# Masked attention of sixteen small heads: the row of maxima leaves between the pairs' stacks, score places chosen by which comes free first, and the outputs of four heads transposed in halves of 64 rows

## The reference, cut to what matters

```python
# the first of eight layers; x is (1, 1024, 256), HEADS = 16, so a head has 16 columns
q = (x @ Wq).reshape(B, T, H, Dh)
k = (x @ Wk).reshape(B, T, H, Dh)
v = (x @ Wv).reshape(B, T, H, Dh)
scores = jnp.einsum('bthd,bshd->bhts', q, k)
mask = jnp.tril(jnp.ones((T, T), dtype=scores.dtype))
scores = scores * mask
attn = jax.nn.softmax(scores / T ** 0.5, axis=-1)
out = jnp.einsum('bhts,bshd->bthd', attn, v).reshape(B, T, H * Dh)
return out @ Wo
...
x = x + _L0_attn_a_ref(_layernorm(x, axis=-1), Wq, Wk, Wv, Wo)   # then seven more layers
```

## Time and profile before

| | us |
|---|---|
| median of 3 runs | 2227.73 (2225.84 to 2228.39) |
| the profiled execution | 2225.98 |
| its span, first to last instruction | 2224.2 |
| the attention layer's last instruction, within the span | about 248 |
| first query unit, first key unit on PE | 41.99, 97.22 |

### The profile page before, as it was taken

How to read it: one execution, slowest core, us unless ns; L and a number is a source line. 1 busy time by engine, 2 the same in 40 slices (tenths; PEclk the granted TensorE clock), 3 DMA queues, 4 the chain that set the end, 5 groups by cost and what they waited for, 6 DMA issues and landing times. The chain is left out here.

```text
span 2224.2 us, 33777 instructions
## 1 busy us (share of the span) xinstructions
PE 1929.2 (87%) x11770; PEld 1552.0 (70%) x11770; DVE 1345.6 (60%) x2478; ACT 936.7 (42%) x1655; POOL 703.4 (32%) x570
## 2 busy tenths in 40 slices
PE   6399799879964667996699999999999999998898
PEld 4144488758841225885588888888888888886687
DVE  4365444655458994346577776767676776674443
ACT  2165343324333323334355554545454554553332
POOL 3001133114348642333433333323233332230132
PEclk9699799889978887997699999999999999999799
DMA  3400013111300002321000000000000000000232
GB/s 80 73 2 2 29 45 108 38 29 53 108 6 0 1 0 85 106 76 52 8 6 11 7 7 10 10 10 10 10 10 10 7 10 10 7 6 15 83 111 78
DMA packets 44908, 73.87 MB, mean 33 GB/s; under 512 B 7360, under 2 KB 27456, under 8 KB 44800
## 3 DMA queue, kind: packets, MB, share of 16 engines
q1 hardware_dynamic: 44800, 72.56, 11.2%
HBM read 64.87 MB, written 1.25 MB: 30 GB/s over the span
## 5 line engine op out<-in xcount | busy, mean ns | idle before, releaser
L791 ACT ACTIVATE gqa_probs<-acc,gqa_bias,gqa_q_scale 128x128 f32<-128x128 f32 (+7 forms) x256 | 212.5, 830 | 274.3 <-DVE gqa_bias L882 274.0
L337 POOL TENSOR_TENSOR f_weighted<-f_hidden,f_comb_all 128x512 f32<-128x512 f32 x128 | 190.5, 1490 | 416.7 <-DVE f_hidden L400 345.1
L1050 PE MATMUL aux<-gqa_probsT,gqa_v 128*128 128x128 f32 x2304 | 306.8, 279 | 1.4 <-ACT gqa_oT L813 1.4
L878 DVE TENSOR_REDUCE gqa_neg_max<-acc 128x1 f32<-128x128 f32 (+7 forms) x256 | 193.7, 757 | 176.4 <-PE acc L1017 165.7
L1050 PEld LDWEIGHTS aux<-gqa_probsT,gqa_v 128*128 128x128 f32 x2304 | 283.7, 195 | 8.2 <-issue 5.1
L734 POOL TENSOR_TENSOR gqa_q_high<-gqa_straight,gqa_turned_q 128x512 fp32r<-128x512 f32 x64 | 81.6, 1275 | 514.7 <-DVE gqa_turned_q L839 514.7
L477 PE MATMUL aux<-xnT_high,f_w_high 128*128 128x512 f32 x512 | 213.8, 418 | 20.6 <-ACT f_silu_g L358 11.1
L400 DVE TENSOR_TENSOR f_hidden<-f_silu_g,aux 128x512 f32<-128x512 f32 x128 | 87.9, 687 | 230.2 <-ACT f_silu_g L358 124.7
L477 PE MATMUL aux<-xnT_low,f_w_high 128*128 128x512 f32 x512 | 210.8, 412 | 0.0
L477 PE MATMUL aux<-xnT_high,f_w_low 128*128 128x512 f32 x512 | 209.9, 410 | 0.0
L1034 PE MATMUL aux<-ident,gqa_probs 128*128 128x128 f32 x1152 | 179.9, 280 | 7.9 <-DVE gqa_probsT L910 4.6
(11 more groups left out here) (330 smaller groups left out, 4325.9 us busy)
## 6 DMA issues: line engine op xcount, KB each, us to landing
f_comb_all<-comb_by_expert SPq DMA_DIRECT2D x48, 512.0 KB, 4.0
f_w<-in_f_up SPq DMA_DIRECT2D x64, 256.0 KB, 3.6
f_w<-in_f_down SPq DMA_DIRECT2D x64, 128.0 KB, 3.8
mat_qk<-mat_high SPq DMA_DIRECT2D x64, 64.0 KB, 2.3
gqa_w_q<-in_g_wq SPq DMA_DIRECT2D x32, 128.0 KB, 2.1
gqa_wo<-in_g_wo SPq DMA_DIRECT2D x32, 128.0 KB, 2.1
mat_qk<-mat_low SPq DMA_DIRECT2D x32, 64.0 KB, 2.3
stream<-in_x SPq DMA_DIRECT2D x1, 1024.0 KB, 5.8
```

The costliest lines, as they stand in the source:

```text
L337: pool.tensor_tensor(weighted[:, j % SLOTS], hidden[:, j % SLOTS], comb_all[:, j // 2 % 2, j % 2 * HALF:(j % 2 + 1) * HALF], ALU.mult).the ...
L791: act.activation(probs[:, j % 4, 0:width(j)], scores(j), ACT.Exp, bias=bias[:, j % 16:j % 16 + 1], scale=q_scale[:, j // NT % 2, tile_of(j ...
L878: dve.tensor_reduce(neg_max[:, j % 16:j % 16 + 1], scores(j), AX, ALU.max, negate=True).then_inc(max_ready, 1)
L1050: last = pe.matmul(aux[:, 2 + t // 4, t % 4 * P:(t % 4 + 1) * P], v[:, g, s, :], probsT[:, j % 4, s * P:(s + 1) * P], start=(s == 0), stop ...
```

## The change

Three things are edited. First, SP issues the stacks of pairs 0 to 2, then waits for the row of pair 0, issues it, issues the stack of pair 3, waits for the row of pair 1, and so on. Second, the function `places()` gives each step the place which, by a small running model of PE, DVE and ACT times, comes free first, and `before` records which step had it. Third, the turning works on halves of 64 rows: 16 transposes of 64 x 128, each with 64 columns of the identity, so that one ACT copy per four heads suffices; the waits on `out_copied` are counted in ones for it.

```diff
     steps = order()
-    slotted = [x for x in steps if x[0] in ("query", "key", "row", "turn", "chunk", "project")]
+    def places():
+
+        place, before, had, left = {}, {}, [None] * 3, [0.0] * 3
+        pe = dve = act = 0.0
+        for kind, n in steps:
+            if kind in ("masked", "weigh"):
+                pe += 0.6
+            if kind == "save":
+                act += 0.6
+            if kind not in ("query", "key", "row", "turn", "chunk", "project"):
+                continue
+            i = left.index(min(left))
+            place[kind, n], before[kind, n], had[i] = i, had[i], (kind, n)
+            pe = max(pe, left[i])
+            if kind == "query":
+                t, c = q_units()[n % UNITS]
+                wide = min((t + 1) * P, (c + 1) * HALF) - c * HALF
+                pe += 0.2 + 0.0004 * wide
+                dve = left[i] = max(dve, pe) + 0.1 + 0.0021 * wide
+            elif kind == "key":
+                b, c = k_units()[n % UNITS]
+                wide = (c + 1) * HALF - max(b * P, c * HALF)
+                pe += 0.2 + 0.0004 * wide
+                act = left[i] = max(act, pe) + 0.2 + 0.0017 * wide
+            else:
+                pe += 0.2 if kind == "row" else 1.0
+                act = left[i] = max(act, pe) + (0.3 if kind == "row" else 1.0)
+        return place, before
...
-        place = {x: i for i, x in enumerate(slotted)}
+        place, before = places()
 
         def slot(kind, n):
-            return slots[place[kind, n] % 3]
+            return slots[place[kind, n]]
...
-            for p in range(PAIRS):
+            def stack(p):
                 sp.wait_ge(low_ready, 2 if p < PAIRS // 2 else 4)
...
+            for p in range(3):
+                stack(p)
             for p in range(PAIRS):
                 sp.wait_ge(row_ready, p + 1)
...
+                if p < PAIRS - 3:
+                    stack(p + 3)
...
-                    for h in range(4):
-                        act.activation(out[:, :, 4 * n + h, :].rearrange("p (c j) d -> p c j d", c=2),
-                                       slot("turn", n)[:, h // 2, :].rearrange("p (j c g d) -> p g c j d", j=4, c=2, g=2)[:, h % 2, :, :, 0:HD0 + 1],
-                                       ACT.Copy).then_inc(out_copied, 1)
+                    act.activation(out[:, :, heads(n), :],
+                                   flat(slot("turn", n)).rearrange("p (t h d) -> p t h d", t=NT, h=4)[:, :, :, 0:HD0 + 1],
+                                   ACT.Copy).then_inc(out_copied, 1)
...
             def free(kind, n):
 
-                i = place[kind, n]
-                if i < 3:
+                if before[kind, n] is None:
                     return
-                was, m = slotted[i - 3]
+                was, m = before[kind, n]
...
-                for t in range(NT):
-                    last = pe.transpose(flat(slot("turn", n))[:, t * P:(t + 1) * P], outT_head[:, t * P:(t + 1) * P], core.ident[:, :])
+                for a in range(2):
+                    for j in range(4):
+                        for c in range(2):
+                            rows = slice(64 * c, 64 * c + 64)
+                            last = pe.transpose(slot("turn", n)[:, c, j * P + 64 * a:j * P + 64 * a + 64],
+                                                outT_head[rows, a * HALF + j * P:a * HALF + (j + 1) * P], core.ident[rows, rows])
```

More of the change, by code:

```diff
@@ L1322, in _ @@
                     break
-                pool.wait_ge(out_copied, 4 * g + 4)
+                pool.wait_ge(out_copied, g + 1)
                 pool.wait_ge(masked_weighed, 2 * g + 2)
@@ L1426, in _ @@
             dve.wait_ge(masked_weighed, 8)
-            dve.wait_ge(out_copied, 16)
+            dve.wait_ge(out_copied, 4)
             dve.tensor_tensor(cut, cut, out[:, :, heads(3), HD0:HD0 + 1].rearrange("p t h a -> p t (h a)"), ALU.add).then_inc(denominator, 1)
@@ L1486, in free @@
                 elif was == "turn":
-                    pe.wait_ge(out_copied, 4 * m + 4)
+                    pe.wait_ge(out_copied, m + 1)
                 elif was == "chunk":
```

## The result

The median fell from 2227.67 (2225.84 to 2228.39, 4 runs) to 2189.12 us (2184.74 to 2190.95, 4 runs): ratio 0.9825 [0.9808, 0.9842]. Forecast were 2195.0 (2188 to 2203) and -32.7 us.

What follows compares the result with a forecast made beforehand. SP's queue was taken to bound the 33.7 us wait, PE the stretch from 106 to 235 us. Terms -32.4 + 0.8 - 0.3 + 0 - 0.6 - 0.2 = -32.7 us gave 2195.0 us, range 2188 to 2203.

Steps and rivals of the forecast that it cites:

- The wait and its cause: First key unit waits 33.7 us for pair 0's row, held in SP's queue; with the row earlier, it starts near 63.6.
- What is late next: After the first key unit, DVE backlog and pair 3's stack together cost 1.2 us; query 23 moves by -32.4 us.
- DVE backlog: Two DVE reductions from 63.44 to 65.25 us; query 20 starts no earlier than that.
- The clock: PE's full clock returns perhaps 4 us of work later, counted from the first key unit: +0.8 us.
- at most 0.36 us: Worth on PE of each microsecond at half the clock, from eight weigh instructions at 1.64 and 1.05 us.
- rival 4: The clock doesn't come back: PE stays at half from the first key units, +40 us, 2268 us; chance 3%.
- The places: Four key units gain 0.7 us each, six queries lose 0.41 us each: -0.3 us; bounds -4.4 and +2.5.
- The turning: Sixteen half transposes cost the same as eight whole ones in each of four turnings: 0, bounds -2.2 to +4.4 us.
- The lower bound, 0.55: Time per turning if two half transposes run side by side and the columns set the time: 0.55 us.
- The copies: One ACT copy of 0.63 us replaces four of 0.81 per turning: -0.6 us on PE's path, -0.2 at the end.
- The sum: All terms together, reaching the layer's end: -32.7 us, median 2195.0 us.
- Rival 3: The places do more: waits for maxima gone (-4.1) and transposes at 0.55 (-2.2), 2188.7 us; chance 9%.

Runs made afterwards that it cites:

- e1_queue: The kernel before with only the new order on SP (stacks of pairs 0 to 2, row 0, stack 3, ...): 2197.74 us, ratio 0.9859.
- e9_own_ring: The changed kernel with exponentials of key units 2 and 3 in memory that no stack is copied from: 2185.28 us, one run.
- e7_swap: The changed kernel with queries 35, 47, 59, 71, 83 and 95 given the place that comes free second: 2187.34 us, ratio 0.9826.
- e2_places: The kernel before with only the new places: 2227.86 us, ratio 0.9998.
- e12_again: The changed kernel once more, with no edit: 2189.05 us, ratio 0.9832.
- e5_act_row: The changed kernel with ACT issuing both row transfers behind its copy and SP issuing all stacks in one loop: 2194.77 us, ratio 0.9857.
- e10_two_first: The changed kernel with only the stacks of pairs 0 and 1 ahead of the row of pair 0: 2196.06 us, one run.
- e4_no_places: The changed kernel with its places going round in turn again: 2191.77 us, ratio 0.9833.
- e8_warm: e5_act_row with two matmuls of zeros on PE behind each of query units 8 to 17: 2195.13 us, ratio 0.9860.
- e11_swap_ring: The changed kernel with the edits of e7_swap and e9_own_ring together: 2186.64 us, ratio 0.9826.
- e3_turning: The kernel before with only the halves of 64 rows and the one copy per turning: 2222.51 us, ratio 0.9981.

## Why the prediction was right, and where a size was off

- **The wait and its cause.** As forecast: the row left at 59.94, the first key unit stood at 62.95 (63.6 forecast) without a wait. e1_queue shows that the order on SP does it alone.
- **What is late next.** Exponential 2 at 70.68 (70.9 forecast), waiting for a transfer; query 23 at 72.46 (72.8), so -32.73 where I had -32.4. The wait for the stack alone costs 1.24 us by e9_own_ring; forecast were 1.2 for it and the DVE backlog together, and the backlog cost nothing that the runs show.
- **The clock.** Forecast +0.8 us, because the small gaps would bring the clock back some 4 us later. In after it came back 7.3 us behind the first key unit where it was 7.1 before, so this cost some 0.1 us and the reason given did not show. But the term is real: in e7_swap the same code up to there got its clock back 13.0 us behind key 0 and paid 1.61 us by query 24. The size in any one execution is luck; the "at most 0.36 us" for each microsecond at half was too low: the runs give 0.45 where exponential 2 has no long wait. Full long before 80 us, and no swing until 200: rival 4 did not come. The section of the Trainium skill named in the prediction, page "TensorE: Matmul & The Clock Gate", has short idle gaps between groups of matmuls as what makes the clock swing. The fall at 56.6 us again follows such gaps (PE busy 1.92 of 3.00 us in 54 to 57), and it did not recur in 88 to 200 us, where PE is busy 107.14 of 112.00.
- **The places.** Forecast -0.3, measured -0.04 between query 24 and key 95 (e2_places): -0.65 and the losses stand at the units that the forecast named, and e7_swap confirms the +0.41. The forecast left out key 1, which now waits for the exponential of key 0; exponential 2 stands 4.20 instead of 3.78 us behind key 0 in e2_places, and this is the likely cause of the 0.2 us at query 24.
- **The turning: the term that was mis-sized.** I took 0, from "eight pairs at the price of eight single ones". The step on PE shrank from 1.02 to 0.53 us, three times in the middle, and at the last turning the copy comes 204.80 - 204.05 = 0.75 us behind the first transpose instead of 240.05 - 238.94 = 1.11: some -1.85 us in all. The lower bound, 0.55, was met, but not quite for its reason: the two halves of a pair do start side by side, half the columns take 0.58 of the time, and the next unit starts 0.17 us sooner behind them, which the sum did not have. The copies were right, 0.62 us instead of 0.81. The Trainium skill, page "TensorEngine Tiling (Array Packing)", section "Key Properties", has the parallel row tiles, and the trace agrees: the halves of a pair start within 0.01 us. By its section "Instruction Overhead" (some 60 cycles for each matmul) half the columns save less than half; the transposes' own steps agree, 0.063 against 0.109 us, and only with the sooner start of the next unit does the whole step come to 0.52 of 1.02.
- **The sum.** Up to layer 2 -36.08 us against the -32.7 forecast: of the 3.4 us between them 1.85 are the transposes, 0.4 the earlier first key unit (34.03 against 33.6), 0.45 the delays and the clock (1.55 against 1.2 + 0.8), 0.24 lie ahead of row 0 and some 0.6 at the layer's end, and the places take 0.3 back. The 0.6 can't be called a gain of the change: the same code took 13.77 us there in one execution and 15.37 in the other (e12_again), at another clock. A further -1.81 us lies in layers whose code did not change. Rival 3's 2188.7 is nearest to the 2189.12 measured, and that is half luck: its transposes came (-1.85 for its -2.2), its places (-4.1) did not, and what makes up for them lies mostly outside the sum.
- **Those layers.** Windows from about 1099 us behind the start of layer 2 to the start of the last layer, after:

```profile
1314.00:2012.32 698.32, 672.11 (x4511) 589.29 (x4511) 470.48 (x1090) 347.98 (x656) 196.76 (x151) 0.96 0.03 9
```

and the same stretch in e12_again, the same kernel:

```profile
1315.30:2008.26 692.96, 667.31 (x4511) 584.99 (x4510) 469.62 (x1088) 347.62 (x654) 195.37 (x149) 0.97 0.03 9
```

and in e2_places:

```profile
1351.00:2053.92 702.92, 679.15 (x4512) 594.01 (x4511) 472.52 (x1092) 349.62 (x656) 198.64 (x152) 0.95 0.03 8
```

The same instructions take 693 to 703 us at a granted clock of 0.97 to 0.95. The two executions of the changed kernel are 5.4 us apart (1797.15 and 1791.72, the second below the 1794 to 1802 that I had expected), so the -1.81 us is within what repeats of one kernel show. Open stays whether part of it is systematic: the three profiles with the old queue have 1798.96, 1801.62 and 1798.15 us from layer 2 to the last, the eleven with the row moved 1791.7 to 1800.9, with a mean some 3 us lower.

## What to carry to other kernels

A transfer whose data are made early can still leave late: compare the line of the trace that makes the data with the line that issues it on its queue, and count what stands between them. When it is moved ahead, what it is moved past becomes the next thing waited for, and its price is the time by which it lands behind its first use, minus what the engines have to do meanwhile. Moving the issue to a compute engine is no way out where that engine's next results are waited for: 2.04 us of issuing on ACT per pair came back as waits of PE. A rule that picks the place which comes free first gains where a unit waited and loses as much where it takes a place just before its reader is done; look at both kinds before expecting anything of it.

## What the runs showed of the hardware that I had not expected

- Half transposes, f32, in rows 0 to 63 and 64 to 127: the two halves start together, a pair takes 0.063 us against 0.109 for a whole one; sixteen halves with the step to the next unit 0.53 us, eight whole ones 1.02.
- The clock falls in some executions where it holds in others, in the same code: in 42 to 54 us the granted clock was 1.00 in before, after and four more executions, 0.86 in two (e5_act_row, e10_two_first) and 0.72 in six (e1_queue to e4_no_places, e8_warm, e11_swap_ring), with PE busy as long:

```profile
42.00:54.00 12.00, 10.75 (x76) 8.03 (x76) 7.10 (x8) 2.23 (x4) 7.15 (x14) 1.00 0.58 102
```

for after, and for e1_queue:

```profile
42.00:54.00 12.00, 10.75 (x57) 7.76 (x57) 6.41 (x7) 1.20 (x2) 7.19 (x15) 0.72 0.60 104
```

Row 0 stands at 58.6 to 59.5 us in the six with the full clock, at 60.4 and 60.9 in the two and at 61.9 to 64.3 in the six. With the new order on SP these three microseconds pass into the whole program; in e2_places and e3_turning, with the old order, they vanish in the wait for the row (key 0 at 97.91 and 97.13, 97.22 before). That is why the pieces of the layer were compared and not the medians.
- When the clock comes back after such a fall differs too, and here it could be priced: some 0.45 us for each microsecond (the table above).
- Two transfers issued by ACT cost 2.04 us of its time, the same two on SP 1.38.
